# A selective state-space layer: the state sum as accumulated turns, the gate in [time, channel], and a new order of the side work

## The reference, cut to what matters

```
x, z  = split(h @ in_proj)                       # 512 channels each
xc    = silu(conv4(x) + conv_b)                  # causal, per channel
dt, B, C = split(xc @ x_proj)                    # B, C: 16 states each
dt    = softplus(dt @ dt_proj + dt_b)
h_t   = exp(dt_t * A) * h_(t-1) + (dt_t * xc_t) * B_t     # per channel and state
y_t   = sum over states of h_t * C_t  +  D * xc_t
out   = (y * silu(z)) @ out_proj
```

## Time and profile before

| | us |
|---|---|
| median of 3 runs | 2798.31 (2797.53 to 2798.88) |
| profiled execution | 2800.64 |
| its span on the device | 2798.8 |
| layer A's units, first scan to last gate | 44.8 to 509.6 |
| layer B's units, first scan to last gate | 1557.9 to 2018.5 |

### The profile page before, as it was taken

How to read it: one execution, slowest core, us unless ns; L and a number is a source line. 1 busy time by engine, 2 the same in 40 slices (tenths; PEclk the granted TensorE clock), 3 DMA queues, 4 the chain that set the end, 5 groups by cost and what they waited for, 6 DMA issues and landing times.

```text
span 2798.8 us, 32693 instructions
## 1 busy us (share of the span) xinstructions
PE 2379.9 (85%) x11300; PEld 1600.5 (57%) x11300; DVE 2118.9 (76%) x3100; ACT 1563.2 (56%) x2734; POOL 1135.3 (41%) x829
## 2 busy tenths in 40 slices
PE   5989896689998798958995798897778987899998
PEld 2333432467776687847884234333333444799998
DVE  5999999699997365538894899999864653577776
ACT  6676574255665455516884866766313444266673
POOL 3889998200000444210221699989601134100004
PEclk9999999899999799979997899999867886799999
DMA  4032040570000000012421330303084231256553
GB/s 178 2 120 92 30 146 0 196 256 1 24 1 1 36 1 31 16 66 95 162 106 53 121 115 7 121 31 102 0 124 103 55 81 58 91 189 224 210 197 95
DMA packets 101607, 247.36 MB, mean 88 GB/s; under 512 B 9285, under 2 KB 65361, under 8 KB 94274
## 3 DMA queue, kind: packets, MB, share of 16 engines
q1 hardware_dynamic: 88530, 222.43, 24.6%
q0 software_dynamic: 5376, 14.70, 1.6%
q10 hardware_dynamic: 7536, 8.13, 1.2%
HBM read 187.96 MB, written 48.81 MB: 85 GB/s over the span
## 4 chain that ended last, share of the span: by engine, by line
PE 42%; DVE 25%; ACT 11%; issue 9%; POOL 9%; DMA 1%; SPq 1%; POOLq 1%; ACTq 1%; DVEq 0%
PE psum L111 7%; DVE psum L758 7%; PE psum L112 7%; PE psum L113 7%; PE psum L498 5%; POOL bu L372 4%; PE psum L118 3%; POOL ch L415 3%; ACT WH L3526 2%; ACT g L3673 2%; DVE ch L775 2%; PE psum L481 2%; DVE ch L758 2%; PE psum L2967 1%; PE psum L2895 1%
## 5 line engine op out<-in xcount | busy, mean ns | idle before, releaser
L372 POOL TENSOR_TENSOR bu<-u,row 128x1024 f32<-128x1024 f32 x254 | 594.8, 2354 | 137.0 <-DVE psum L758 47.5
L498 PE MATMUL psum<-ch,ident 128*128 128x512 f32 x1024 | 513.2, 634 | 114.6 <-DVE ch L775 63.7
L758 DVE TENSOR_TENSOR_SCAN psum<-psum,bu 128x1024 f32<-128x1024 f32 x210 | 479.8, 2285 | 22.1 <-ACT psum L590 21.2
L498 PEld LDWEIGHTS psum<-ch,ident 128*128 128x128 f32 x1024 | 190.4, 198 | 401.6 <-issue 184.1
L590 ACT ACTIVATE psum<-dt,A 128x511 f32<-128x511 f32 x512 | 332.1, 681 | 0.4
L775 DVE TENSOR_TENSOR ch<-psum,row 128x1024 f32<-128x1024 f32 x210 | 256.6, 1222 | 5.7
L3673 ACT ACTIVATE g<-psum,bias 128x256 f32<-128x256 f32 x248 | 101.1, 470 | 133.8 <-PE psum L113 129.6
L3495 POOL DMA_INDIRECT R<-m1res,gi x26 | 26.2, 1006 | 340.3 <-DMA m1res<-ob 324.2
L462 PE MATMUL psum<-hT,inw 128*128 128x512 f32 x256 | 130.0, 637 | 27.9 <-ACT xs L536 20.6
L111 PE MATMUL psum<-WH,hs 128*128 128x256 f32 x496 | 144.8, 292 | 5.0 <-DVE hs L3753 2.2
L111 PE MATMUL psum<-xT,WH 128*128 128x256 f32 x496 | 142.0, 286 | 7.6 <-DVE xT L3716 7.6
(11 more groups left out here) (456 smaller groups left out, 6536.7 us busy)
## 6 DMA issues: line engine op xcount, KB each, us to landing
W<-in_m1W SPq DMA_DIRECT2D x24, 2052.0 KB, 8.5
row<-Ascr SPq DMA_DIRECT2D x64, 512.0 KB, 5.7
row<-Bscr SPq DMA_DIRECT2D x64, 512.0 KB, 5.8
m1buf<-zt SPq DMA_DIRECT2D x8, 2048.0 KB, 17.0
W<-in_m0W SPq DMA_DIRECT2D x16, 1024.0 KB, 5.9
m1res<-ob ACTq DMA_DIRECT2D x23, 256.0 KB, 4.9
m0buf<-zt SPq DMA_DIRECT2D x2, 2064.0 KB, 18.0
xe<-m0buf SPq DMA_DIRECT2D x8, 516.0 KB, 8.0
```

What stands on the lines that cost most here:

```text
L372: e.tensor_tensor(m.bu[i % 3][:, :, :], u, m.row[:, g, 0, :, :], ALU.mult).then_inc(*m.fed.up)
L498: p = pe.matmul(m.y, k.ident, m.ch[i % RING_C][:, j, :], start=False, stop=g == UNITS - 1 and j == 1)
L758: dve.tensor_tensor_scan(to, flat, m.bu[i % 3][:, :, :].rearrange("p a n -> p (a n)"), 0.0, ALU.mult, ALU.add).then_inc(*m.scan.up)
```

## The change

The sum: instead of two products of 512 columns with the identity stationary, eight turns of 128x128 (the `ch` tile stationary, the identity moving, marked as transposes) are added up in `y`, which now holds [time, channel]. The D term is a ScalarE multiplication into `dx` and four more turns. So `z` is computed in [time, channel] too, the gate multiplies there, and the gated tile `yzT` is turned back by a new item `yt` (four turns, drawn by ScalarE) before `out`. TensorE's sum of unit i - 1 now stands at the head of turn i, ahead of the items, and ScalarE draws all items one turn later than they are issued. The gate moves from g == 0 to g == 1.

GpSimd meets C in units g = 1 and 5 of every group (8 of 32 in every batch). The ring of `bu` shrinks from three buffers to two: the input of unit i + 2 waits for the scan of unit i, no longer i - 1. Channel group 0's convolution becomes a TensorE item, with its diagonals in `dg0`. `z` moves from the end of the batch before (n = 26 to 30) into the batch's own turns 2, 4, 6 and 7, with one silu of 2048 columns at turn 8; the convolutions move to n = 17, 18, 20, 21, their silu to 22, `xp` to 23, `dt` to 24 to 27, softplus to 26 and 28, and the last of the four `mamba_dt` to the next batch's turn 0. `FROM_PE` is empty, so every branch on `from_pe` is idle, and so is the item `bt`.

```diff
+FROM_PE = ()
+BY_POOL = (1, 5)
...
-    m.tap = al([128, T], "tap")
+    m.dg0 = al([128, 4, 128], "dg0")
...
-    m.sz, m.xc, m.dt = al([128, SIX, T], "sz"), al([128, SIX, T], "xc"), al([128, SIX, T], "dt")
+    m.sz, m.xc, m.dt = al([128, 4, T], "sz"), al([128, SIX, T], "xc"), al([128, SIX, T], "dt")
     m.u = [al([128, T], "u") for _ in range(2)]
+    m.yzT, m.dx = al([128, 4, 128], "yzT"), al([128, T], "dx")
...
-    m.bu = [al([128, 2, T], "bu") for _ in range(3)]
+    m.bu = [al([128, 2, T], "bu") for _ in range(2)]
...
-OPENING = {0: ("z", 0), 1: ("z", 1), 2: ("z", 2), 3: ("z", 3)}
-BEFORE = {2: ("out", 0), 3: ("out", 1), 4: ("out", 2), 5: ("out", 3)}
-AHEAD = {6: ("h", 0), 7: ("h", 1), 8: ("in", 0), 9: ("in", 1), 11: ("in", 2), 12: ("in", 3),
-         14: ("conv", 1), 16: ("conv", 2), 18: ("conv", 3),
-         21: ("xp", 0), 22: ("dt", 0), 23: ("dt", 1), 24: ("dt", 2), 25: ("dt", 3),
-         26: ("z", 0), 28: ("z", 1), 29: ("z", 2), 30: ("z", 3)}
+FIRST_BANKS = (0, 1, 2, 3, 4, 5, 6, 7, 0, 1, 3, 6)
+OWN = {2: ("z", 0), 4: ("z", 1), 6: ("z", 2), 7: ("z", 3), 13: ("yt", 0), 19: ("yt", 1), 28: ("yt", 2)}
+BEFORE = {1: ("yt", 3), 3: ("out", 0), 5: ("out", 1), 8: ("out", 2), 11: ("out", 3)}
+AHEAD = {9: ("h", 0), 10: ("h", 1), 12: ("in", 0), 14: ("in", 1), 15: ("in", 2), 16: ("in", 3),
+         17: ("conv", 0), 18: ("conv", 1), 20: ("conv", 2), 21: ("conv", 3),
+         23: ("xp", 0), 24: ("dt", 0), 25: ("dt", 1), 26: ("dt", 2), 27: ("dt", 3)}
...
+        o.append((OWN[s][0], b, OWN[s][1]))
...
-    return n % UNITS in (2, 5) and (b == B - 1 or n in (2, 5, 18, 21, 26))
+    return from_pe(i) or i % UNITS in BY_POOL
...
+    if n >= 2:
+        e.wait_ge(*m.scan(FED[n - 2]))
...
-        if b + 1 < B and 9 <= n < 16:
-            mamba_conv_pool(k, m, pool, b + 1, n - 9)
+        if n == 0 and b:
+            mamba_dt(k, m, pool, 4 * b + 3)
+        if 29 <= n and b + 1 < B:
+            if n == 29:
                 pool.wait_ge(*m.soft(3 * b + 6))
-            mamba_dt(k, m, pool, 4 * (b + 1) + n - 28)
-        if n % UNITS == 4 and i // UNITS + 1 < 4 * B:
+            mamba_dt(k, m, pool, 4 * (b + 1) + n - 29)
+        if n in (4, 12, 20) or n == 29 and b + 1 < B:
...
+    elif w == "z":
+        for f in range(2):
+            p = pe.matmul(bank, m.hT[:, f, 128 * j:128 * j + 128], m.inw[:, f, T:2 * T], start=f == 0, stop=f == 1)
+    elif w == "yt":
+        pe.wait_ge(*m.gated(4 * b + j))
+        for c in range(4):
+            p = turn_in(k, pe, bank[:, 128 * c:128 * c + 128], m.yzT[:, c, :])
...
+def mamba_sum_pe(k, m, pe, i):
+
+    s, g = i // UNITS, i % UNITS
+    if g == 0:
+        if s:
+            pe.wait_ge(*m.gated(s - 1))
+        pe.wait_ge(*m.dx_in(s))
+        for c in range(4):
+            p = pe.matmul(m.y[:, c, :], m.dx[:, 128 * c:128 * c + 128], k.ident, start=c == 0, stop=False, is_transpose=True)
+        p.then_inc(*m.direct.up)
+    pe.wait_ge(*mamba_out(m, i))
+    for j in range(2):
+        for c in range(4):
+            p = pe.matmul(m.y[:, c, :], m.ch[i % RING_C][:, j, 128 * c:128 * c + 128], k.ident, start=False,
+                          stop=g == UNITS - 1 and j == 1 and c == 3, is_transpose=True)
+    p.then_inc(*m.summed.up)
 
-        s, g = i // UNITS, i % UNITS
+        if i:
+            mamba_sum_pe(k, m, pe, i - 1)
         for item in mamba_items(i):
             mamba_item_pe(k, m, pe, *item)
-        if g == 0:
-            pe.wait_ge(*(m.gated(s - 1) if s else m.diag(1)))
-            pe.matmul(m.y, m.dg[:, 12 + s % 4, :], m.xc[:, s % SIX, :], start=True, stop=False).then_inc(*m.direct.up)
-        pe.wait_ge(*mamba_out(m, i))
-        for j in range(2):
-            p = pe.matmul(m.y, k.ident, m.ch[i % RING_C][:, j, :], start=False, stop=g == UNITS - 1 and j == 1)
-        p.then_inc(*m.summed.up)
+    mamba_sum_pe(k, m, pe, PER * B - 1)
+    mamba_item_pe(k, m, pe, "yt", B - 1, 3)
...
+def mamba_direct_act(k, m, act, s):
+
+    act.wait_ge(*m.xc_in(s))
+    if s:
+        act.wait_ge(*m.direct(s - 1))
+    act.activation(m.dx[:, :], m.xc[:, s % SIX, :], ACT.Identity, scale=pv(k, m.L + "D", 4)[:, s % 4:s % 4 + 1]).then_inc(*m.dx_in.up)
...
-            if item[0] == "conv":
-                mamba_item_act(k, m, act, *item)
-        for item in mamba_items(i):
-            if item[0] != "conv":
-                mamba_item_act(k, m, act, *item)
+            mamba_item_act(k, m, act, *item)
+        if i in (8, 9):
+            for j in range(8) if i == 8 else range(4):
+                o, n0 = (m.dg, 4) if i == 8 else (m.dg0, 0)
+                g = act.activation(o[:, j, :], k.ident, ACT.Identity, scale=cw[:, n0 + j:n0 + j + 1])
+            g.then_inc(*m.diag.up)
+        if n == 14 and b:
             x_stats_act(k, act, 4 * (m.rnd + 1) + b - 1)
-        if n == (2 if b else 4):
+        if n == 8:
             mamba_gate_act(k, m, act, b)
-        if n == 5 and b + 1 < B:
+        if n == 6 and b + 1 < B:
             mamba_rows_act(k, m, act, b + 1)
-        if n == 19 and b + 1 < B:
+        if n % UNITS == 3 and i // UNITS + 1 < 4 * B:
+            mamba_direct_act(k, m, act, i // UNITS + 1)
+        if n == 22 and b + 1 < B:
             mamba_silu_act(k, m, act, b + 1)
-        if n in (24, 25) and b + 1 < B:
-            mamba_soft_exp_act(k, m, act, b + 1, 2 * (n - 24), 2 * (n - 24) + 2)
-        if n == 26 and b + 1 < B:
+        if n in (26, 28) and b + 1 < B:
+            mamba_soft_exp_act(k, m, act, b + 1, n - 26, n - 24)
+        if n == 28 and b + 1 < B:
             mamba_soft_log_act(k, m, act, 3 * b + 5, 0, 4)
+    mamba_item_act(k, m, act, "yt", B - 1, 3)
...
-        if b:
-            dve.wait_ge(*m.full(mamba_use("out", b - 1, 3)))
-    dve.tensor_tensor(m.yz[:, db, :], m.y, m.sz[:, s % SIX, :], ALU.mult).then_inc(*m.gated.up)
+    if s:
+        dve.wait_ge(*m.full(mamba_use("yt", (s - 1) // 4, (s - 1) % 4)))
+    dve.tensor_tensor(m.yzT[:, :, :], m.y, m.sz[:, :, 128 * db:128 * db + 128], ALU.mult).then_inc(*m.gated.up)
...
-        if g == 0 and s:
+        if g == 1 and s:
```

More of the change, by code:

```diff
@@ L232, in mamba_make @@
     m.spilled = c(L + "B_C_spilled", B, 16)
-    m.rows = [c(L + f"B_C_rows{i}", 2 * B, 16) for i in range(UNITS)]
-    m.decay, m.fed, m.scan, m.summed = (c(L + s, n) for s in ("decay", "input", "scan", "y_summed"))
+    m.rows = [c(L + f"B_C_rows{i}", B if i in FROM_PE else 2 * B, 16) for i in range(UNITS)]
+    m.decay, m.scan, m.summed = (c(L + s, n) for s in ("decay", "scan", "y_summed"))
+    m.fed = c(L + "input", len(FED))
     m.out = c(L + "h_C", n - MET[n])
     m.met = c(L + "h_C_pool", MET[n])
-    m.diag = c(L + "diagonals", 2)
-    m.direct = c(L + "D_x", 4 * B)
+    m.diag = c(L + "diagonals", 3)
+    m.dx_in, m.direct = c(L + "x_times_D", 4 * B), c(L + "D_x", 4 * B)
     m.gated = c(L + "gated", 4 * B)
@@ L269, in mamba_uses @@
         o += mamba_items(i)
-    return o + [("out", B - 1, j) for j in range(4)]
+    return o + [("yt", B - 1, 3)] + [("out", B - 1, j) for j in range(4)]
 USE = {u: n for n, u in enumerate(mamba_uses())}
@@ L279, in mamba_use, with from_pe @@
     return USE[w, b, j]
+def from_pe(i):
+    return i % UNITS in FROM_PE
+FED = [i for i in range(PER * B) if not from_pe(i)]
+FED_PE = [i for i in range(PER * B) if from_pe(i)]
+NTH = {i: n for a in (FED, FED_PE) for n, i in enumerate(a)}
 def by_pool(i):
-    b, n = i // PER, i % PER
-    return n % UNITS in (2, 5) and (b == B - 1 or n in (2, 5, 18, 21, 26))
+    return from_pe(i) or i % UNITS in BY_POOL
 MET = [sum(by_pool(j) for j in range(i)) for i in range(PER * B + 1)]
@@ L337, in mamba_sp @@
                 sp.wait_ge(*mamba_out(m, PER * (b - 1) + 3 * UNITS + g))
-            for j in range(2):
+            for j in (1,) if g in FROM_PE else range(2):
                 sp.dma_start(m.row[:, g, j, :, :], m.scr[b, 16 * j + 2 * g:16 * j + 2 * g + 2, :].partition_broadcast(128)) \
@@ L414, in mamba_met_pool @@
     pool.wait_ge(*m.scan(i))
+    if from_pe(i) and i // UNITS % 4 == 0:
+        pool.wait_ge(*m.rows[i % UNITS](i // PER))
     pool.tensor_tensor(o, o, m.row[:, i % UNITS, 1, :, :], ALU.mult).then_inc(*m.met.up)
@@ L424, in mamba_pool @@
         b, n = i // PER, i % PER
-        if i + 2 < PER * B:
+        if i + 2 < PER * B and not from_pe(i + 2):
             mamba_input(k, m, pool, i + 2)
@@ L449, in mamba_item_pe @@
     elif 8 <= n < LEAD:
-        pe.wait_ge(*m.drawn(n - 8))
+        pe.wait_ge(*m.drawn(6))
     if w == "h":
@@ L466, in mamba_item_pe @@
             pe.wait_ge(*m.drawn(mamba_use("in", 0, j)))
+        elif b == 1 and j == 0:
+            pe.wait_ge(*m.diag(2))
+        elif b == 1 and j == 1:
+            pe.wait_ge(*m.diag(1))
         for f in range(4):
-            p = pe.matmul(bank, m.dg[:, 4 * (j - 1) + f, :], m.xs[:, j, f:f + T], start=f == 0, stop=f == 3)
+            p = pe.matmul(bank, m.dg[:, 4 * (j - 1) + f, :] if j else m.dg0[:, f, :], m.xs[:, j, f:f + T], start=f == 0, stop=f == 3)
     elif w == "xp":
```

(32 more changed lines are left out.)

97 lines of the change are left out of this document (35 added, 62 removed).

## The result

| | before | after |
|---|---|---|
| median of the runs on one chip | 2798.6 us | 2856.1 us (2854.4 to 2869.3, 4 runs) |
| profiled execution, its span | 2800.6, 2798.8 | 2854.4, 2852.2 |
| granted clock over the span | 0.916 | 0.867 |
| layer A, first to last scan | 458.5 us | 487.9 us |
| layer B, the same | 454.3 us | 481.2 us |

The ratio is 1.0212 (95%: 1.0178 to 1.0245). Between the profiled executions, from a layer's first scan to the end of its last addition to X, layer A grew by 30.2 us and layer B by 27.8, and the rest of the kernel gives 4.6 back. The forecast was 2813 with a range of 2778 to 2850.

A forecast was written before the change was run, and what follows sets the result against it. VectorE was taken to set the pace, GpSimd and TensorE close behind. Terms -22.7 - 57.8 + 51.0 + 16.6 + 11.0 + 2.2 + 2.6 + 12 = +14.9 us gave 2813 us, range 2778 to 2850.

The forecast's parts named there:

- 18 products off VectorE: Three more units' products with C in each layer's first three batches go to GpSimd, 1.26 us each: -22.7 us.
- scan 25, silu of the convolution: At batch boundaries, scan 25 waits for ScalarE's silu and decays behind convolution 3: 4.5 us late, six times.
- end of batch, two buffers: At six batch boundaries, GpSimd's inputs come late to the next batch's units 0, 2 and 4: 4.0 us each.
- opening: At each layer's start, scan 2 waits 5.5 us for its decays: 11.0 us in two layers.
- gate's silu: Gate after scan 9 waits for ScalarE's silu: 1.4 us in six batches, 4.1 in each layer's first: 16.6 us.
- gate of the third group: VectorE's gate in a batch's third group: the prediction put in no wait, 0 us.
- additions to X inside the loops: VectorE's additions to X within the two layers' loops: waits struck out and none put in, 0 us.
- last gates: At each layer's end, the last gate waits 1.1 us for one sum: 2.2 us.
- ends: `yt` 3 and low clock: At layer ends, `yt` 3 and its draw before `out` cost 2.6 us, sums and items at the low clock 12.
- all 57.8 us are struck out first: VectorE's waits inside the two loops of the kernel before, removed whole before walking the new order's waits: -57.8 us.
- Rival 1: TensorE falls to its low level inside the batches: 66 us if always, 33 in half the places, 2846; chance 0.20.
- Rivals 2, 3 and 4: 2: queues slide, waits hidden, 2779, chance 0.22; 3: no change, 2798, 0.13; 4: adding turns take two records, 2854, 0.03.

The follow-up runs named there:

- warm: The changed kernel with four bf16 products of zeros added into y ahead of each sum's wait, except a group's first unit: 2851.5 us, 1.0194 to the kernel before.
- order2: The change with three bu buffers, in at 12 to 15, convolutions 16 to 19, first dx after unit 2's decays: 2793.9 us; order2_warm adds two zero products per unit: 2784.2 us.
- before_share: The kernel before with GpSimd's product with C in 8 units of 32 in every batch, nothing else: 2851.0 us, 1.0189.

## Why the prediction was wrong
Its terms against the trace, both layers, in us:

| step | forecast | measured |
|---|---|---|
| 18 products off VectorE | -22.7 | -21.7 busy |
| scan 25, silu of the convolution | 27.0 | 29.3 |
| end of batch, two buffers | 24.0 | about 27 |
| opening | 11.0 | 10.6 |
| gate's silu | 16.6 | 30.1 |
| gate of the third group | 0 | 7.3 |
| additions to X inside the loops | 0 | 14.8 |
| last gates | 2.2 | 4.5 |
| ends: `yt` 3 and low clock | 14.6 | about 3 |

With -22.7 - 57.8 the measured waits (126.6) sum to +46; the profiled executions differ by 53.4 in span. The groups by line also hold the waits of some tenths that the table leaves out: all waits of scans, gates and additions grew from 69.8 to 143.9 us, and 74.1 - 22.7 = 51.4. The layers grew by 58.0; the other 6.6 fit a batch's work, which was 106.9 us in the second and third batches where 106.0 (109.8 less three units) was counted, and 4.6 came back outside the layers.

*Right.* The direction, and two walks within a tenth, scan 25 and the opening. The boundary's sum (24.0 against about 27) is near by luck: all of it was to be waits for GpSimd's inputs, which took some 12, and scan 31 behind softplus took 14.7, which the walk had hidden under those inputs. Unit 0 of a batch waited at most 1.4 us, not 2.4. The direction, too, is right with help: less the 24.0 us of the ring the forecast would have been 9 us faster than before, and three_bu, the change without the smaller ring, is 10 us slower (2807.8 against 2797.4).

*The step that failed* is "The gate's and the additions' waits go too ... So all 57.8 us are struck out first, and what the new order makes VectorE wait for is put in", together with the price of the ring in "The end of a batch". The ring was walked only where a scan waits for an input, once per batch, 4.0 us. It works in every group of eight: the input of i+2 and the product of i wait for the same scan, so the product of GpSimd is 2.3 us late, and TensorE's sum, `z`, `out` and with them silu, gate and X stand behind it. The terms of gates and additions (gate's silu, third group, additions inside the loops, last gates) were 18.8 us and measured 56.7; with three buffers the same places wait 27.5. The ring alone is +55 us in the old kernel (before_two_bu) and some -48 us when given back (three_bu), of which 43 lie in the two layers of the profiled executions; the end-of-batch term had it at 24. The gate's walk did have "input of 7 first", and at the full clock it holds (1.2 us in warm); the same line was not walked for `out` and X.

*Rival 1*, the low level inside the batches: its condition came true in part (0.95 to 0.81 over layer A), its price did not, and that its 2846 is nearer to the result than the forecast is luck. (The prediction calls it "the second rival below" where it names the page; the low level is the first of its list.) It was set at 33 to 66 us; at gates and additions it is some 13, and warm's net gain of 5 lies within the error. The Trainium skill, "TensorE: Matmul & The Clock Gate", section "Part 4: PE-mode transpose", has turns not counting as activity; the fall of the clock with turns, and its return to 0.93 with the same sums as products, agree with it. That the full clock does not engage for turns does not hold word for word here: sums of eight turns took 1.04 us amid products, half of the low level's 1.92 to 1.97.

*The ends* were charged 2.6 us for `yt` 3 and 12 for the low clock. The first charge was right: the first addition after a layer waits 3.48 us instead of 2.09, 2.8 in both layers. The second did not come. The last 24 turns were at the low level for part of their time (8 in 1.43 us, granted clock 0.65), which is in the last gates' 4.5, but the four `out` items behind them took 7.17 us, as in the kernel before, at a granted clock of 1.00. First the clock of the last batch and of its last turns, then the instructions:
```profile
461.20:537.80 76.60, 41.26 (x224) 36.56 (x224) 73.46 (x54) 36.12 (x72) 62.57 (x28) 0.73 0.04 14
533.45:537.80 4.35, 4.30 (x24) 4.06 (x24) 2.12 (x3) 0.00 (x0) 0.00 (x0) 0.65 0.00 0
```
```profile
533.45 4.30 PE L502 MATMUL psum<-ident,ch 128*128 128x128 f32 x24 [5.82 <-POOL ch L404]
...
539.93 7.17 PE L485 MATMUL psum<-outw,yz 128*128 128x256 f32 x32 [0.67 <-ACT yz L558]
```
What was charged does exist in another order: in order2 the same four items take 9.55 us, and the first addition waits 5.73.
```profile
508.77 9.55 PE L485 MATMUL psum<-outw,yz 128*128 128x256 f32 x32 [0.67 <-ACT yz L558]
```
A mean over a batch said nothing about its last ten microseconds. Why the level returned there in the one kernel and not in the other is open.

*Rivals 2, 3 and 4.* The waits did not slide away; even with the third buffer and another order (order2) the kernel was only 0.2% below the one before. The result was not "no change" either. Rival 4 is refuted by the records (2048 against the 4096 of products).

*Open.* How before_share's +54 us divides between late inputs and late sums, and what the clock costs with two buffers apart from the queue time of the zero products: no run takes the one without the other.

## What to carry over
A buffer taken out of a ring costs more than the consumer's wait: ask which other work of that engine waits for the same event, what stands behind that work in the next in-order engine, and walk all of it, not only the boundary. A wait seen at a gate may be moved from instruction to instruction without a gain; find the release that two pieces of work share. Spare time of TensorE can be filled with zero products to hold its clock, but they stand in its queue as well: two per unit gained 12 us with three buffers, four with two buffers nothing that could be measured. Two with two buffers, or four with three, were not run.

## What the runs showed of the hardware
- fp32 turns that add up in PSUM are one record each: eight in 1.04 to 1.10 us at the full level (2.4 GHz), 1.92 to 1.97 at the low one (1.2 GHz); as ordinary products sixteen records take 1.95 us at the full level.
- Layer A's granted clock, 44 to 510 us: 0.95 before, 0.81 with turns, 0.93 with the same sums as products, 0.91 with four zero bf16 products per unit; in the order of order2 0.80, and 0.89 with two per unit (order2_warm).
- Behind idle time the level drops for single instructions: after 3.07 us without work the sum took 1.09 us and `z` 2 behind it 3.55, after 2.43 us the sum took 1.97 and `z` 0 2.42; with zeros ahead of the sum (warm) the same two `z` took 1.88 each.
